# Attention's inverse row sums reach their rows through a small table in device memory

## The chip, the cores and the metric

The kernel runs on one core of one Trainium2 chip. The metric is the time of one execution on the device in microseconds (us), the median of the runs made. An engine here is one of TensorE (PE, whose weight loads are listed apart as PEld), VectorE (DVE), ScalarE (ACT), GpSimd (POOL) and SyncE (SP), which issues nearly all plain DMAs.

## The reference, cut to what matters

A cross attention with eight heads, over channels of 64 rows, and then a mixture of experts. The change is in the attention alone.

```
def _L0_xattn_ref(q, k, v, gamma):          # B, 512, 512 each; q is the normed x, k = v = context
    qh, kh, vh = (a.reshape(B, 8, 64, 512) for a in (q, k, v))
    qk = einsum('bhdq,bhdl->bhql', qh, kh) / sqrt(64)
    sm = softmax(qk, axis=-1)
    ret = einsum('bhql,bhdl->bhdq', sm, vh).reshape(B, 512, 512)
    return gamma * ret
x = x + _L0_xattn_ref(layernorm(x), ctx, ctx, gamma)
x = x + ffn(layernorm(x), ...)              # shared expert, router, top 2 of 8 experts
```

The softmax is computed without its division: each query's exponentials are multiplied with the values, and the result is multiplied by the inverse of that query's sum (and by gamma) afterwards. The queries of a result are its columns, in the free dimension, while the sums come out with the queries on the partitions. So 512 inverse sums for each head have to be turned from columns into rows and repeated over the 64 rows of the head.

## The kernel before, in words

The rows of x (2048) are cut into 16 tiles of 128 rows, two heads each. The first stage handles one tile in one step; the loop is `step(i)`, written once for each engine, with i from -4 to 18, and each engine runs its own list in order, with semaphores between them. Several tiles are in flight in a step: PE computes the scores of tile i and the start of i+1 (`scores`, L1295), transposes the exponentials (`probs_T`, L1315), multiplies them by the values in a high and a low part (`times_v`, L1323), and transposes the normed result of tile i-3 for the router (`rows_T`, L1351, and `logits`, L1357). ACT computes the exponentials (`exps`, L717) and copies the transposed ones out of PSUM (`probs_hi`, L724); DVE takes maxima (L986), the low parts (`probs_lo`, L997) and adds the two halves of a result (`halves`, L1001). POOL splits queries and keys into high and low parts, scales the attention's result (`scaled`, L572) and adds it to x (`residual`, L578). After the 16 tiles come the shared expert (L1428 to 1467) and the 39 slots of the routed experts.

The sums of tile t travel like this. DVE inverts them (`inverse`, L991: `rinv`, 128 partitions with 4 chunks of queries by 2 heads). POOL's `spread(t)` (L566) repeats each of the 8 columns 64 times into `rspr`, 128x512. PE's `inverses(t)` (L1338) transposes it in four pieces of 128x128 into PSUM bank `bT[1]`; in PE's list it stands in step t+1 between the third and the fourth `times_v` of the tile. ACT's `inverses(t)` (L729) copies the bank to `rgam`, with the factor gamma. POOL's `scaled(t)` (L572) waits for it and for DVE's `halves`, and multiplies `att` by `rgam`.

`bT[1]` is shared: `freed(...)` (L1288) makes PE wait for the latest reader of the bank that it will overwrite, and `a_Rg` is ACT's signal after its copy.

SP's list in a step: store the normed rows of tile i-3 (L355), load context i+2 (L347), store the transposed rows i-3 (L359), load x i+4 (L342), store x2 of tile i-1 (L351), and in some steps load weight chunks (L371) or a block of four transposed tiles (`load_block`, L374, 1 MB). In step 16 (i == NT) POOL also makes the high and low parts of weight chunk 1 (`first_weights`, L584), ahead of `scaled(15)`.

Of the kernel before, what the change touches and what calls it, by code (L numbers as in the profile page):

```python
# [5 lines left out]
ALU = mybir.AluOpType  # L6
ACT = mybir.ActivationFunctionType
AX_X = mybir.AxisListType.X
F32 = mybir.dt.float32
# [8 lines left out]
def xattn_moe_kernel(nc, x, ctx_in, gamma, router_w, w_gate, w_up, w_down, sw_gate, sw_up, sw_down, shared_gate_w, out):  # L18
# [49 lines left out]
    xn_d = nc.dram_tensor("x2_normed_rows", (T + P, H), F32, kind="Internal").ap()  # L68
    xT_d = nc.dram_tensor("x2_normed_transposed", (NT, P, H), F32, kind="Internal").ap()
    meta_d = nc.dram_tensor("slot_rows", (SLOTS * P, 2), I32, kind="Internal").ap()  # L70

    ctx = ExitStack()
    with ctx:
        def sem(name):
            return ctx.enter_context(nc.semaphore(name))
# [61 lines left out]
        att = [place(f"att{j}", [P, L]) for j in range(2)]  # L137
        rspr = place("rspr", [P, 2 * QC, DH])
        rgam = place("rgam", [P, L])
# [100 lines left out]

        e_s, d_max, a_exp, d_rinv, g_rspr, e_R, a_Rg = sem("e_s"), sem("d_max"), sem("a_exp"), sem("d_rinv"), sem("g_rspr"), sem("e_R"), sem("a_Rg")

# [53 lines left out]
        def there(t):  # L296

            return not isinstance(t, int) or 0 <= t < NT
# [39 lines left out]
        def _(sp):  # L338
# [14 lines left out]
            def store_normed(t):  # L353
                sp.wait_ge(g_x2n, t + 1)
                sp.dma_start(xn_d[0:T, :].rearrange("(t p) h -> t p h", p=P)[t, :, :], x2n[t % 2][:, :]).then_inc(st_x2n[t % 2], 16)  # L355

            def store_columns(t):
                sp.wait_ge(a_x2T, t + 1)
                sp.dma_start(xT_d[t, :, :], x2T[t % 2][:, :, :].rearrange("p c t -> p (c t)")).then_inc(st_x2T[t % 2], 16)  # L359
# [35 lines left out]
            def step(i):  # L395
                if there(i - 3):
                    store_normed(i - 3)
                if there(i + 2):
                    load_values(i + 2)
                if there(i - 3):  # L400
                    store_columns(i - 3)
                if there(i + 4):
                    load_x(i + 4)
                if i == NT:
                    load_chunk(3)
                if there(i - 1):
                    store_rows(i - 1)
                if i == 2:
                    pads()
                if i == 3:  # L410
                    load_chunk(0)
                if i == 5:
                    load_chunk(1)
                if i == 7:
                    load_block(0, 0)
                if i == 10:
                    load_chunk(2)
                if i == NT - 1:
                    load_block(1, 1)
# [72 lines left out]
        def _(g):  # L492
# [72 lines left out]

            def spread(t):  # L566

                g.wait_ge(d_rinv, t + 1)
                after(g, e_R, t)
                gp.tensor_copy(rspr[:, :, :], rinv[:, :, :].rearrange("p c s -> p (c s)").unsqueeze(2).to_broadcast([P, 2 * QC, DH])).then_inc(g_rspr, 1)  # L570

            def scaled(t):  # L572

                g.wait_ge(d_att, 2 * t + 2)
                g.wait_ge(a_Rg, t + 1)
                gp.tensor_tensor(att[t % 2][:, :], att[t % 2][:, :], rgam[:, :], ALU.mult).then_inc(g_att, 1)
# [23 lines left out]
            def step(i):  # L600
                if there(i + 1):
                    queries(i + 1)
                if there(i + 1) and i + 1 > 0:
                    keys_hi(i + 1)
                    queries_hi(i + 1)
                if there(i - 3):
                    rows_normed(i - 3)
                if i == NT:

                    g.wait_ge(e_s, 8 * NT)  # L610
                    g.wait_ge(e_vt, NT)
                    for n in range(3):
                        first_weights(1, n)
                if there(i + 1) and i + 1 > 0:
                    queries_lo(i + 1)
                    keys_lo(i + 1)
                if 6 <= i < 9:
                    first_weights(0, i - 6)
                if 9 <= i < 9 + TB:
                    first_tokens(i - 9)  # L620
                if there(i - 2):
                    inverse_deviation(1, i - 2)
                if there(i + 2):
                    inverse_deviation(0, i + 2)
                if there(i):
                    spread(i)
                if there(i + 2):
                    shift(0, i + 2)
                if there(i - 1):
                    scaled(i - 1)  # L630
                if there(i - 2):
                    shift(1, i - 2)
                if there(i - 1):
                    residual(i - 1)
# [73 lines left out]
        def _(act):  # L708
# [19 lines left out]

            def inverses(t):  # L729

                act.wait_ge(e_R, t + 1)
                after(act, g_att, t)
                sc.activation(rgam[:, :], bT[1][:, :], ACT.Copy, scale=gam[:, :]).then_inc(a_Rg, 1)

            def low_half(t, s):
# [29 lines left out]
            def step(i):  # L765
# [7 lines left out]
                if there(i - 1):  # L773
                    probs_hi(i - 1, 4)
                    inverses(i - 1)
                    low_half(i - 1, 0)
                    probs_hi(i - 1, 5)
# [178 lines left out]
        def _(dve):  # L956
# [34 lines left out]
            def inverse(t):  # L991

                dve.wait_ge(a_exp, 8 * t + 8)
                after(dve, g_rspr, t)
                ve.reciprocal(rinv[:, :, :], rsum[:, :, :]).then_inc(d_rinv, 1)
# [289 lines left out]
        def _(pe):  # L1285
# [51 lines left out]

            def inverses(t):  # L1338

                pe.wait_ge(g_rspr, t + 1)  # L1340
                for c in range(QC):
                    ins = te.transpose(bT[1][:, c * P:(c + 1) * P], rspr[:, 2 * c:2 * c + 2, :].rearrange("p s d -> p (s d)"), ident[:, :])
                ins.then_inc(e_R, 1)

            def values_T(t, half, par):
# [25 lines left out]
            def step(i, half, par):  # L1371
                if there(i - 1):
                    freed((d_ptl, 8, i - 1, 2), (d_ptl, 8, i - 1, 0), (d_ptl, 8, i - 2, 6), (d_ptl, 8, i - 2, 4))
                    probs_T(i - 1, 1 - par, 4)
                    times_v(i - 1, 1 - par, 2)
                    freed((d_vl, 1, i, 0), (d_ptl, 8, i - 1, 1), (a_x2T, 1, i - 4, 0), (a_Rg, 1, i - 2, 0))
                    inverses(i - 1)
                    times_v(i - 1, 1 - par, 3)
# [7 lines left out]
                if there(i - 3):  # L1386
                    freed((a_Rg, 1, i - 1, 0), (d_vl, 1, i, 0), (d_ptl, 8, i - 1, 1), (a_x2T, 1, i - 4, 0))
                    rows_T(i - 3, 1 - par)
# [14 lines left out]
                if there(i):  # L1403
                    freed((a_x2T, 1, i - 3, 0), (a_Rg, 1, i - 1, 0), (d_vl, 1, i, 0), (d_ptl, 8, i - 1, 1))
                    probs_T(i, par, 1)
# [10 lines left out]
                if there(i + 1):  # L1416
                    freed((d_ptl, 8, i, 1), (a_x2T, 1, i - 3, 0), (a_Rg, 1, i - 1, 0), (d_vl, 1, i, 0))
                    values_T(i + 1, half + par, 1 - par)
# [89 lines left out]
            gate_up(0, 0, 0)  # L1508
            pe.wait_ge(a_Rg, NT)
            rows_T(NT - 2, 0)  # L1510
# [97 lines left out]
```

## Time and profile before

| | before |
|---|---|
| runs | 876.71, 878.79, 879.09 us |
| median | 878.79 us |
| profiled execution, its own time | 879.82 us |
| profiled execution, its span | 878.1 us |
| PE, DVE, ACT, POOL busy in the span | 97%, 65%, 57%, 51% |
| the attention's steady step, from one tile's `inverses` on PE to the next | 13.6 us |

The span reaches from the first to the last instruction of the profiled execution; 1.7 us of that execution's time lie around it. The first stage lasts to about 240 us of the span. The busy time of PE is modelled with the whole duration of each matmul, while matmuls overlap, so the distance from start to start tells more than the busy share.

### The profile page before, as it was taken

The numbers are of one execution on the slowest core, as the hardware profiler recorded it, in microseconds if no ns is written. First come the engines' busy times: TensorE is split into PE (matmuls) and PEld (weight loads), VectorE is DVE, ScalarE is ACT, GpSimd is POOL, SyncE is SP. The second block draws the span as 40 slices with busy tenths as digits, with TensorE's granted clock in tenths as the row PEclk, the third lists the DMA queues.
The fourth block names the chain that finished last, engine by engine and source line by source line (L and its number), as shares of the span: only waits on it lengthen the run. The fifth ranks groups of instructions, "written<-read, shape, count | busy, mean of one in ns | idle before, by whom it ended". The sixth has DMA issues, their size and how long they took to land.

```text
span 878.1 us, 13766 instructions
## 1 busy us (share of the span) xinstructions
PE 849.9 (97%) x4624; PEld 708.6 (81%) x4624; DVE 566.7 (65%) x820; ACT 503.4 (57%) x861; POOL 447.3 (51%) x430
## 2 busy tenths in 40 slices
PE   6999999999999999999999999999999999999993
PEld 3677777777788888888888888888899999999992
DVE  6999999999656414321212121118899999999991
ACT  4899999999653211211111111116788888888881
POOL 5576888875700000144330000003899999999974
PEclk9999999999999999999999999999999999999997
DMA  3124442321453382001320023547744443443442
GB/s 96 61 91 138 133 143 97 132 84 61 156 161 93 85 49 96 1 2 33 112 26 1 0 97 106 191 159 265 216 84 77 85 80 72 81 86 72 76 69 36
DMA packets 63237, 81.24 MB, mean 93 GB/s; under 512 B 15370, under 2 KB 34826, under 8 KB 63187
## 3 DMA queue, kind: packets, MB, share of 16 engines
q1 hardware_dynamic: 53426, 60.14, 22.7%
q0 software_dynamic: 9760, 20.49, 13.1%
q8 instruction: 25, 0.41, 0.2%
q14 instruction: 26, 0.20, 0.1%
HBM read 53.01 MB, written 27.60 MB: 92 GB/s over the span
## 4 chain that ended last, share of the span: by engine, by line
PE 92%; POOL 2%; issue 1%; DMA 1%; DVE 1%; ACT 1%; POOLq 0%; ACTq 0%; DVEq 0%
PE scores L1450 9%; PE scores L1451 9%; PE scores L1452 9%; PE scores L1311 7%; PE bank L1320 6%; PE bank L1464 5%; PE bank L1465 5%; PE bank L1466 5%; PE bank L1334 4%; PE bank L1336 3%; PE bank L1564 3%; PE bank L1565 3%; PE bank L1566 3%; PE bank L1533 3%; PE bank L1535 3%; PE bank L1534 3%
## 5 line engine op out<-in xcount | busy, mean ns | idle before, releaser
L1091 DVE TENSOR_TENSOR sg<-scores,sg 128x512 f32<-128x512 f32 x44 | 30.4, 692 | 201.3 <-PE scores L1452 201.2
L1450 PE MATMUL scores<-x_hl,wsp 128*128 128x512 f32 x352 | 137.2, 390 | 0.0
L1452 PE MATMUL scores<-x_hl,wsp 128*128 128x512 f32 x352 | 137.0, 389 | 0.0
L1451 PE MATMUL scores<-x_hl,wsp 128*128 128x512 f32 x352 | 137.0, 389 | 0.0
L644 POOL DMA_INDIRECT slot_rows<-msrc,posi x32 | 36.1, 1129 | 170.7 <-PE scores L1452 164.3
L659 POOL DMA_INDIRECT xg<-x_normed_rows,meta x39 | 38.5, 988 | 160.0 <-PE scores L1474 141.6
L815 ACT ACTIVATE sg<-scores 128x512 f32<-128x512 f32 x44 | 26.3, 598 | 158.4 <-PE scores L1452 158.4
L822 ACT ACTIVATE hh<-sg 128x512 fp32r<-128x512 f32 x44 | 27.8, 632 | 115.0 <-DVE sg L1091 100.0
L999 DVE TENSOR_TENSOR ptl<-bank,pth 128x512 fp32r<-128x512 f32 x128 | 87.3, 684 | 8.6 <-ACT pth L727 8.1
L721 ACT ACTIVATE pb<-scores,negmax 128x512 f32<-128x512 f32 x128 | 88.1, 694 | 4.6 <-DVE negmax L989 4.6
L727 ACT ACTIVATE pth<-bank 128x512 fp32r<-128x512 f32 x128 | 76.7, 600 | 12.3 <-PE bank L1320 11.1
L685 POOL TENSOR_TENSOR wd<-wex,wd 96x512 fp32r<-96x512 f32 x38 | 79.3, 2087 | 3.2
L1320 PEld LDWEIGHTS bank<-ident,pb 128*128 128x128 f32 x512 | 61.2, 142 | 23.8 <-issue 9.8
L1320 PE MATMUL bank<-ident,pb 128*128 128x128 f32 x512 | 79.7, 280 | 0.2 <-DVE ptl L999 0.2
L989 DVE TENSOR_REDUCE negmax<-scores 128x2 f32<-128x1024 f32 x64 | 77.8, 1215 | 2.9 <-PE scores L1311 2.9
L1452 PEld LDWEIGHTS scores<-x_hl,wsp 128*128 128x128 f32 x352 | 66.1, 188 | 13.8
L1450 PEld LDWEIGHTS scores<-x_hl,wsp 128*128 128x128 f32 x352 | 66.1, 188 | 13.7
L1451 PEld LDWEIGHTS scores<-x_hl,wsp 128*128 128x128 f32 x352 | 66.1, 188 | 13.6
L670 POOL DMA_INDIRECT out<-y,meta x39 | 64.8, 1662 | 16.1 <-DMA out<-y,meta 9.5
L1207 DVE TENSOR_TENSOR wg<-wex,wg 128x1408 fp32r<-128x1408 f32 x39 | 63.5, 1628 | 12.6 <-ACT wg L868 12.5
L1464 PE MATMUL bank<-wsp,hh 128*128 128x512 f32 x176 | 68.8, 391 | 0.8 <-DVE tot_s L1161 0.6
L1466 PE MATMUL bank<-wsp,hl 128*128 128x512 f32 x176 | 68.5, 389 | 0.0
(197 smaller groups left out, 2228.0 us busy)
## 6 DMA issues: line engine op xcount, KB each, us to landing
wex<-in_L_ffn_w_gate SPq DMA_DIRECT2D x8, 704.0 KB, 4.4
wex<-in_L_ffn_w_up SPq DMA_DIRECT2D x8, 704.0 KB, 5.8
xb<-in_x SPq DMA_DIRECT2D x16, 256.0 KB, 2.8
cn<-in_ctx SPq DMA_DIRECT2D x16, 256.0 KB, 2.8
x_rows<-xb SPq DMA_DIRECT2D x16, 256.0 KB, 2.0
x_normed_rows<-x2n SPq DMA_DIRECT2D x16, 256.0 KB, 2.0
x_normed_transposed<-x2T SPq DMA_DIRECT2D x16, 256.0 KB, 2.0
x_hl<-x_normed_transposed SPq DMA_DIRECT2D x4, 1024.0 KB, 5.3
```

Of the source, the lines that this page charges most:

```text
L670: g.indirect_dma_start(out=out, out_offset=bass.IndirectOffsetOnAxis(ap=meta[:, s, 0:1], axis=0), in_=y3[s % 2][:, :], in_offset=None, com ...
L685: gp.tensor_tensor(w[0:IR, 1, c], wex[0:IR, e, 2 * W3 + (IC - 1) * H:EW], w[0:IR, 0, c].bitcast(F32), ALU.subtract).then_inc(g_wd, 1)
L721: sc.activation(pb[t % 2][s][:, c, :], bSS[c % 2][:, s, :], ACT.Exp, bias=negmax[:, c, s:s + 1], scale=1.0, accum_out=rsum[:, c, s:s + 1]) ...
L727: sc.activation(pth[n % 4][:, :], bT[P_BANK[n]][:, :], ACT.Copy).then_inc(a_pth, 1)
L989: ve.tensor_reduce(negmax[:, c, :], bSS[c % 2][:, :, :], AX_X, ALU.max, negate=True).then_inc(d_max, 1)
L999: ve.tensor_tensor(ptl[n % 4][:, :], bT[P_BANK[n]][:, :], pth[n % 4][:, :].bitcast(F32), ALU.subtract).then_inc(d_ptl, 1)
L1320: ins = te.transpose(bT[P_BANK[n]][:, q * P:(q + 1) * P], pb[par][s][:, q, c * P:(c + 1) * P], ident[:, :])
L1450: te.matmul(bk[:, :], hi, xhi, start=(h == 0), stop=False)
L1451: te.matmul(bk[:, :], hi, xlo, start=False, stop=False)
L1452: ins = te.matmul(bk[:, :], lo, xhi, start=False, stop=(h == HC - 1))
L1464: te.matmul(bY[tt][:, :], th, hi, start=(c == 0), stop=False)
L1466: ins = te.matmul(bY[tt][:, :], tl, hi, start=False, stop=(c == SC - 1))
```

## The change

POOL's `spread` becomes `inverses(t)`: one instruction that multiplies the 128x8 inverse sums by gamma into `rgs`. SP stores `rgs` into a table in device memory, `inverse_sums`, with two DMAs for a tile (one for each head, 128 partitions by 4 words, each word going to another place 512 bytes on), and later reads a head's 512 words back as one row, repeated over 64 partitions of `rgam`, with two more DMAs. PE's four transposes, ACT's copy and the waits on `a_Rg` go. The table has two halves, for even and odd tiles.

```diff
+    inv_d = nc.dram_tensor("inverse_sums", (2, 2, L), F32, kind="Internal").ap()
...
-        rspr = place("rspr", [P, 2 * QC, DH])
+        rgs = place("rgs", [P, QC, 2])
...
+            def store_inverses(t):
+
+                sp.wait_ge(g_rgs, t + 1)
+                after(sp, g_att, t - 1)
+                for s in range(2):
+                    sp.dma_start(inv_d[t % 2, s, :].rearrange("(c p) -> p c", p=P), rgs[:, :, s], allow_slow_non_contiguous=True).then_inc(st_inv, 16)
+
+            def load_inverses(t):
+                sp.wait_ge(st_inv, 32 * (t + 1))
+                after(sp, g_att, t)
+                for s in range(2):
+                    sp.dma_start(rgam[DH * s:DH * (s + 1), :], inv_d[t % 2, s, :].partition_broadcast(DH)).then_inc(ld_inv, 16)
...
                 if there(i + 2):
                     load_values(i + 2)
+                if there(i - 1):
+                    load_inverses(i - 1)
                 if there(i - 3):
                     store_columns(i - 3)
                 if there(i + 4):
                     load_x(i + 4)
+                if there(i):
+                    store_inverses(i)
...
-            def spread(t):
+            def inverses(t):
 
                 g.wait_ge(d_rinv, t + 1)
-                after(g, e_R, t)
-                gp.tensor_copy(rspr[:, :, :], rinv[:, :, :].rearrange("p c s -> p (c s)").unsqueeze(2).to_broadcast([P, 2 * QC, DH])).then_inc(g_rspr, 1)
+                after(g, st_inv, 32 * t)
+                if t == 0:
+                    g.wait_ge(ld_small, 48)
+                gp.tensor_scalar(rgs[:, :, :], rinv[:, :, :], gam[:, :], None, ALU.mult).then_inc(g_rgs, 1)
...
                 g.wait_ge(d_att, 2 * t + 2)
-                g.wait_ge(a_Rg, t + 1)
+                g.wait_ge(ld_inv, 32 * (t + 1))
                 gp.tensor_tensor(att[t % 2][:, :], att[t % 2][:, :], rgam[:, :], ALU.mult).then_inc(g_att, 1)
...
-                sc.activation(rgam[:, :], bT[1][:, :], ACT.Copy, scale=gam[:, :]).then_inc(a_Rg, 1)
...
-                    ins = te.transpose(bT[1][:, c * P:(c + 1) * P], rspr[:, 2 * c:2 * c + 2, :].rearrange("p s d -> p (s d)"), ident[:, :])
...
-                    freed((d_vl, 1, i, 0), (d_ptl, 8, i - 1, 1), (a_x2T, 1, i - 4, 0), (a_Rg, 1, i - 2, 0))
-                    inverses(i - 1)
                     times_v(i - 1, 1 - par, 3)
...
-            pe.wait_ge(a_Rg, NT)
```

PE's list before, in a step of the first stage (L1320 is `probs_T`, L1334 and L1336 the two matmuls of one `times_v`, L1342 `inverses`, L1311 `scores`):

```order
L1334 MATMUL bank<-pth_97,vs_90 128x512 [waits a_pth]
L1336 MATMUL bank<-ptl_101,vs_90 128x512 [waits d_ptl]
L1342 MATMUL bank<-ident,rspr 128x128 [waits g_rspr,d_vl]
L1342 MATMUL bank<-ident,rspr 128x128 x3
L1334 MATMUL bank<-pth_98,vs_90 128x512 [waits a_pth]
L1336 MATMUL bank<-ptl_102,vs_90 128x512 [waits d_ptl]
L1320 MATMUL bank<-ident,pb_94 128x128 [waits d_ptl]
```

The same place in the changed kernel (L1334 is now `probs_T`, L1348 and L1350 `times_v`):

```order
L1348 MATMUL bank<-pth_97,vs_90 128x512 [waits a_pth]
L1350 MATMUL bank<-ptl_101,vs_90 128x512 [waits d_ptl]
L1348 MATMUL bank<-pth_98,vs_90 128x512 [waits a_pth]
L1350 MATMUL bank<-ptl_102,vs_90 128x512 [waits d_ptl]
L1334 MATMUL bank<-ident,pb_94 128x128 [waits d_ptl]
```

The four transposes and their wait are gone, and two `times_v` follow each other. Nothing else moves on PE.

SP's list before, at the end of the first stage (from `store_rows(14)` in step 15 on):

```order
L351 DMA x_rows<-xb_87 128x512 [waits g_x2]
L378 DMA x_hl<-x_normed_transposed 128x4x512 [waits st_x2T1,st_x2T0]
L355 DMA x_normed_rows<-x2n_109 128x512 [waits g_x2n]
L359 DMA x_normed_transposed<-x2T_111 128x512 [waits a_x2T]
L371 DMA stg_126<-in_L_ffn_sw_gate 128x4x128 [waits g_wl]
```

The same stretch in the changed kernel, from the two stores of tile 15 on:

```order
L364 DMA inverse_sums<-rgs 128x4x1 [waits g_att,g_rgs]
L364 DMA inverse_sums<-rgs 128x4x1
L353 DMA x_rows<-xb_87 128x512 [waits g_x2]
L393 DMA x_hl<-x_normed_transposed 128x4x512 [waits st_x2T1,st_x2T0]
L357 DMA x_normed_rows<-x2n_109 128x512 [waits g_x2n]
L370 DMA rgam<-inverse_sums 64x512 [waits g_att,st_inv]
L370 DMA rgam<-inverse_sums 64x512
L374 DMA x_normed_transposed<-x2T_111 128x512 [waits a_x2T]
```

The table's loads stand behind the 1 MB load of `x_hl` and the store of the normed rows. In the other steps they stand behind the load of the context, and the stores of the next tile a step's half later, behind the load of x.

## Rows read from the trace of the kernel before

**Rows 1.** The page: span, busy times, and PE's granted clock in 40 slices.
```profile
span 878.1 us, 13766 instructions
...
PE 849.9 (97%) x4624; PEld 708.6 (81%) x4624; DVE 566.7 (65%) x820; ACT 503.4 (57%) x861; POOL 447.3 (51%) x430
...
PEclk9999999999999999999999999999999999999997
```
**Rows 2.** Busy times by stretch (us): PE, PEld, DVE, ACT, POOL, PEclk, DMA share, GB/s.
```profile
120.00:140.00 20.00, 20.00 (x137) 15.00 (x135) 19.27 (x33) 18.34 (x43) 17.72 (x22) 1.00 0.46 157
```
**Rows 3.** The chain that ended last, 120 to 123 us: start, us, what.
```profile
120.90 0.23 PE bank L1336
121.14 0.44 PE bank L1342 x4
121.57 0.23 PE bank L1334
121.81 0.24 PE bank L1336
122.04 0.44 PE bank L1320 x4
```
**Rows 4.** PE's timeline where two `times_v` follow each other: start, us, what.
```profile
225.65 0.39 PE L1336 MATMUL bank<-ptl,vs 128*128 128x512 f32 x1
225.88 0.39 PE L1334 MATMUL bank<-pth,vs 128*128 128x512 f32 x1
226.11 0.40 PE L1336 MATMUL bank<-ptl,vs 128*128 128x512 f32 x1
```
**Rows 5.** All transposes of L1342: duration ns min/median/max, first and last start.
```profile
L1342 PE MATMUL bank<-ident,rspr x64: 271/272/273, 26.2 to 227.7; 128*128 128x128 f32 x64
```
**Rows 6.** The chain where it leaves PE, at the stage's end.
```profile
224.31 0.71 DVE att L1006
225.09 1.30 POOL att L576
```
**Rows 7.** ACT's and DVE's timeline in a steady step, with their idle time before.
```profile
121.61 0.69 ACT L733 ACTIVATE rgam<-bank,gam 128x512 f32<-128x512 f32 x1 [0.31 <-PE bank L1342]
122.32 0.60 ACT L740 ACTIVATE lob<-bank 64x512 f32<-64x512 f32 x1
...
122.95 0.68 DVE L1006 TENSOR_TENSOR att<-bank,lob 64x512 f32<-64x512 f32 x1 [0.17 <-ACT lob L740]
...
128.43 0.69 DVE L999 TENSOR_TENSOR ptl<-bank,pth 128x512 fp32r<-128x512 f32 x1 [0.35 <-ACT pth L727]
```
**Rows 8.** POOL's timeline in the same step, and the scores that wait for its keys.
```profile
122.92 1.28 POOL L557 TENSOR_TENSOR kl<-cn,kh 128x512 fp32r<-128x512 f32 x1
...
125.70 0.50 PE L1311 MATMUL scores<-kh,qh 64*128 64x512 f32 x2
...
128.15 0.61 POOL L570 COPY rspr<-rinv 128x512 f32<-128x512 f32 x1 [0.21 <-DVE rinv L995]
...
128.75 0.26 POOL L528 TENSOR_SCALAR nmr<-aggr,rstd 128x1 f32<-128x1 f32 x1
...
129.94 1.28 POOL L576 TENSOR_TENSOR att<-att,rgam 128x512 f32<-128x512 f32 x1 [0.93 <-DVE att L1006]
```
**Rows 9.** DMA issues of the page: KB each, median us from issue to landing.
```profile
cn<-in_ctx SPq DMA_DIRECT2D x16, 256.0 KB, 2.8
...
x_normed_rows<-x2n SPq DMA_DIRECT2D x16, 256.0 KB, 2.0
...
x_hl<-x_normed_transposed SPq DMA_DIRECT2D x4, 1024.0 KB, 5.3
...
slot_rows<-meta SPq DMA_DIRECT2D x1, 39.0 KB, 17.5
```
**Rows 10.** SP's issues, steady (135.83) and at the stage's end.
```profile
135.83 0.35 SPq L347 DMA_DIRECT2D cn<-in_ctx  x1
...
228.32 1.03 SPq L378 DMA_DIRECT2D x_hl<-x_normed_transposed  x1
229.39 0.51 SPq L355 DMA_DIRECT2D x_normed_rows<-x2n  x1
```
**Rows 11.** Landing of the store issued at 229.39: min/median/max.
```profile
DMA to landing us min/median/max: 5.7/5.7/5.7
```
**Rows 12.** The chain at the stage's end, from POOL back to PE.
```profile
234.91 1.26 POOL att L576
...
239.17 0.77 POOL x2n L564
240.08 0.63 PE bank L1354 x4
```

More of the change, by code:

```diff
@@ L239, in xattn_moe_kernel @@
         e_vt, a_vh, d_vl = sem("e_vt"), sem("a_vh"), sem("d_vl")
-        e_s, d_max, a_exp, d_rinv, g_rspr, e_R, a_Rg = sem("e_s"), sem("d_max"), sem("a_exp"), sem("d_rinv"), sem("g_rspr"), sem("e_R"), sem("a_Rg")
+        e_s, d_max, a_exp, d_rinv, g_rgs = sem("e_s"), sem("d_max"), sem("a_exp"), sem("d_rinv"), sem("g_rgs")
+        st_inv, ld_inv = sem("st_inv"), sem("ld_inv")
         e_t, a_pth, d_ptl, e_pv = sem("e_t"), sem("a_pth"), sem("d_ptl"), sem("e_pv")
@@ L625, in step @@
                 if there(i):
-                    spread(i)
+                    inverses(i)
                 if there(i + 2):
@@ L727, in probs_hi @@
                 sc.activation(pth[n % 4][:, :], bT[P_BANK[n]][:, :], ACT.Copy).then_inc(a_pth, 1)
-            def inverses(t):
-                act.wait_ge(e_R, t + 1)
-                after(act, g_att, t)
-                sc.activation(rgam[:, :], bT[1][:, :], ACT.Copy, scale=gam[:, :]).then_inc(a_Rg, 1)
             def low_half(t, s):
@@ L993, in inverse @@
                 dve.wait_ge(a_exp, 8 * t + 8)
-                after(dve, g_rspr, t)
+                after(dve, g_rgs, t)
                 ve.reciprocal(rinv[:, :, :], rsum[:, :, :]).then_inc(d_rinv, 1)
@@ L1336, in times_v @@
                 te.matmul(bO[:, :], v, ptl[n % 4][:, :], start=False, stop=(c == LC - 1)).then_inc(e_pv, 1)
-            def inverses(t):
-                pe.wait_ge(g_rspr, t + 1)
-                for c in range(QC):
-                    ins = te.transpose(bT[1][:, c * P:(c + 1) * P], rspr[:, 2 * c:2 * c + 2, :].rearrange("p s d -> p (s d)"), ident[:, :])
-                ins.then_inc(e_R, 1)
             def values_T(t, half, par):
@@ L1375, in step @@
                     times_v(i - 1, 1 - par, 2)
-                    freed((d_vl, 1, i, 0), (d_ptl, 8, i - 1, 1), (a_x2T, 1, i - 4, 0), (a_Rg, 1, i - 2, 0))
-                    inverses(i - 1)
                     times_v(i - 1, 1 - par, 3)
@@ L1386, in step @@
                 if there(i - 3):
-                    freed((a_Rg, 1, i - 1, 0), (d_vl, 1, i, 0), (d_ptl, 8, i - 1, 1), (a_x2T, 1, i - 4, 0))
+                    freed((d_vl, 1, i, 0), (d_ptl, 8, i - 1, 1), (a_x2T, 1, i - 4, 0))
                     rows_T(i - 3, 1 - par)
@@ L1403, in step @@
                 if there(i):
-                    freed((a_x2T, 1, i - 3, 0), (a_Rg, 1, i - 1, 0), (d_vl, 1, i, 0), (d_ptl, 8, i - 1, 1))
+                    freed((a_x2T, 1, i - 3, 0), (d_vl, 1, i, 0), (d_ptl, 8, i - 1, 1))
                     probs_T(i, par, 1)
@@ L1416, in step @@
                 if there(i + 1):
-                    freed((d_ptl, 8, i, 1), (a_x2T, 1, i - 3, 0), (a_Rg, 1, i - 1, 0), (d_vl, 1, i, 0))
+                    freed((d_ptl, 8, i, 1), (a_x2T, 1, i - 3, 0), (d_vl, 1, i, 0))
                     values_T(i + 1, half + par, 1 - par)
```

## The prediction

> **What bounds the kernel now.** I read the page first. PE is busy for 97% of the span and its clock is granted in full but for the last slice [rows 1], so the change can only pay through PE's own list, or cost by making PE wait. The view by stretches says the same of the stage that is changed: in 20 us of the first stage PE is busy for 20.00, DVE for 19.27, ACT for 18.34 and POOL for 17.72, at clock 1.00 [rows 2]. The reader should see two things there: PE is full, and DVE is nearly full behind it. Third, the chain that ended last: in steady steps it stays on PE from matmul to matmul, the four transposes of L1342 among them, with 0.44 us [rows 3]. It stays there until DVE's `halves` at 224.31, which hands it to POOL [rows 6], and comes back to PE with `rows_T` at 240.08 [rows 12]. From there on PE works through both expert stages, in which the change touches nothing.
>
> **What is removed from PE.** The transposes are 64 matmuls of 0.272 us [rows 5], 17.4 us of busy time, but matmuls overlap. What counts is how much later the next one starts. With the transposes, the chain gets from the start of the L1336 before them (120.90) to that of the L1334 behind them (121.57) in 0.67 us, of which L1336 has 0.23 and the four transposes 0.44 [rows 3]. Where two `times_v` follow each other without transposes, their starts are 0.23 apart, and 0.23 again [rows 4]. So taking the four out gives 0.44 per tile, and nothing is left in their place.
>
> The Trainium skill (TensorE: Matmul & The Clock Gate, Part 4: PE-mode transpose) gives about 275 ns for a 128x128 transpose in one kernel's context. The trace agrees with that as a duration (0.272), but by it as a price the 60 transposes on the path would give an estimated 16.5 us; the chain prices them at 0.11 each.
>
> The transposes of tiles 0 to 14 are on the path. Those of tile 15 start after 224.31, where the chain has left PE, and give nothing. Gain: 15 x 0.44 = **6.6 us**.
>
> **Can the others follow?** The steady step is 13.6 us and would become 13.2. ACT loses its copy of 0.69 and the idle 0.31 before it [rows 7], 1.0 us in all against 0.44: it follows with ease. DVE loses nothing. In one step it waits twice, 0.17 before `halves` and 0.35 before the first `probs_lo` [rows 7], 0.52 in all, so it can follow 0.44 and has 0.08 left, if both gaps can close. The first one waits for ACT's `lob`, which stood right behind the removed copy (its end is at 122.30, `lob` starts at 122.32), so it closes. The second waits for ACT behind PE's own transposes of the exponentials, which come 0.44 earlier. I therefore take the full 0.44; the bound below is a step that shortens by the 0.17 alone, 15 x 0.17 = 2.6 us.
>
> **POOL.** 0.61 for the spread becomes a small tensor_scalar over 8 words a partition; the nearest rows are 0.26 (one word) and 0.61 (512 words) [rows 8]. Either way it costs nothing: POOL waits 0.93 us for DVE two instructions later [rows 8]. If that cover went, POOL would still be no later than before.
>
> **The DMAs, steady steps.** A tile issues four: two stores of 512 words and two loads of 128 KB. On SP an issue takes 0.35 [rows 10], 1.4 us of a 13.6 us step, between waits for other engines: hidden. The trace has one DMA in which each descriptor moves a few bytes: `slot_rows<-meta`, 39 KB in pieces of 8 bytes, 4992 of them, 17.5 us to landing; a store of 256 KB in long rows lands after 2.0 [rows 9]. So a piece costs (17.5 - 2.0) / 4992, and 1024 words give 2.0 + 3.2 = 5.2 us. The bounds for the pair are 2.0 and 17.5.
>
> How much time is there? The stores can be issued when the inverse sums are scaled, about 128.45 (128.15 plus 0.3). `load_inverses` stands in SP's next step behind the context's load at 135.83 [rows 10]: 7.4 us for 5.2, so SP hardly waits. The table is wanted by `scaled` one step after 129.94, at 143.56 [rows 8]; a load issued at 136.2 and landing like the context's in 2.8 [rows 9] is there at 139. Queued behind SP's new waits are the store of the transposed rows, the next x (four steps ahead) and the x2 store, none of which is wanted before the next step. Cost: 0, and 4.5 us remain as cover.
>
> **The DMAs, at the stage's end.** Here they are not covered. In step 16 the loads stand behind the 1 MB of `x_hl`, issued at 228.32, and the store at 229.39 [rows 10], and that store took 5.7 us instead of 2.0: it landed at 235.1 [rows 11, 9]. The two table loads come behind it. `scaled(15)` starts at 234.91 with POOL busy up to there, and through `residual` and x2n it releases PE's `rows_T` at 240.08 [rows 12]: what it is late there, PE is late. The extra 256 KB at the rate between the 2.8 us of 256 KB and the 5.3 us of 1 MB [rows 9] are 0.85 us, so landing is at about 236.0 and the cost is **1.1 us**. Bounds: 0, if the loads pass the store, and 235.1 + 2.8 - 234.9 = 3.0. I take 1.1, as the row of the delayed store is the nearest.
>
> **Sum.** Against the profiled execution: 879.8 - 6.6 + 1.1 = 874.3 us. That execution is 1.0 us above the median of the runs shown, 878.79; on the median's scale the forecast is **873.3 us**, 0.63% less. A measurement of this kernel tells about 0.3% from no change, which is 2.6 us: 876.2 to 881.4 counts as the same.
>
> **The rivals.**
>
> *DVE takes PE's place (0.20).* For: DVE is busy 19.27 of 20 us [rows 2], and only 0.08 us a step would remain. If the 0.35 gap doesn't close, for it is latency through ACT, the step shortens by 0.17: 878.8 - 2.6 + 1.1 = 877.3, within 0.3%. If neither closes, 879.9. Against: both gaps end at instructions that come earlier with the change.
>
> *The table comes late in every step (0.12, slower).* The place is `scaled`. The mechanism is the price of single words. From 128.45 to 143.56 there are 15.1 us, of which the load needs 2.8, and POOL may be about 1.5 later before PE feels it: its keys end at 124.2 and the scores that need them start at 125.70 [rows 8]. It decides when the stores take over 13.8 us. If each took the 17.5 us of the only row with scattered pieces, the table would be 5.2 us late and PE 3.7, x 15 tiles = 56 us: 878.8 + 56 = 935 us. Against it: that row moves five times as many pieces. The Trainium skill (DMA: Bandwidth & Descriptors, Rules for kernel authors) has a non-contiguous last dimension lowered to one descriptor per element, and calls a plain DMA with a rearranged pattern 19 times slower than a hardware transpose. The 17.5 us row agrees with the first in kind; an estimate by the second, 19 x 2.0 = 38 us a store, would put this rival far above 935. No row here shows such a factor for 512 words.
>
> *Every transpose held PE for its whole duration (0.02).* Then 60 x 0.272 = 16.3 us go: 878.8 - 16.3 + 1.1 = 863.6. The spacing of 0.44 for four speaks flatly against it [rows 3]. It is how the skill's page, named above, would be read.
>
> The forecast keeps 0.66. That the change would not do what it says can be left out: PE's list shows the transposes gone.
>
> **How the numbers follow.** Faster by over 0.3%: 0.66 + 0.02 = 0.68. Within 0.3%: 0.20. Slower: 0.12. The range must leave out no more than 2 in 10: it leaves out the late table (0.12) and the 863.6 (0.02), and a little at each end. Its low end is the full gain without the cost at the stage's end, 878.8 - 6.6 = 872.2, less the 1.2 us by which such medians scatter: 871.0. Its high end takes in the case of DVE with as little scatter: 878.0.
>
> **What would show it.** Right: the distance between one tile's `scores` and the next falls from 13.6 to 13.2 us; the chain stays on PE; DVE's idle time in a step falls to about 0.1; the stores' landing is near 5 us; `scaled(15)` waits for a DMA by about 1 us. Wrong: a step of 13.4 or more with DVE or ACT as the releaser of PE; `scaled` waiting for `rgam`'s DMA in the steady steps; store landings over 12 us; or SP late with the context, so that keys wait.

## The result, and the profile after

The changed kernel takes **894.29 us** (median of 4 runs, 893.46 to 898.59) against 877.89 us for the kernel before beside it: a ratio of **1.0197** [1.0177, 1.0217], 16.4 us slower. The forecast was 5.5 us faster, so its sign is wrong. 894.29 lies outside the range and between "same" and the 935 us of the rival in which the table comes late.

The page of the changed kernel (its profiled execution took 894.19 us). The rows on span, busy times and clock answer to [rows 1]; the others are the busy tenths of PE and of the DMA engines, the packets, the chain by engine, and the DMA issues with their median landing:

```profile
span 892.4 us, 13684 instructions
...
PE 846.9 (95%) x4560; PEld 702.9 (79%) x4560; DVE 565.8 (63%) x820; ACT 492.9 (55%) x845; POOL 438.2 (49%) x430
...
PE   6998998999979999999999999999999999999993
...
PEclk9999999999989999999999999999999999999997
DMA  3466666664663293000211012556944344344442
...
DMA packets 82691, 85.49 MB, mean 96 GB/s; under 512 B 32777, under 2 KB 52233, under 8 KB 82642
...
PE 76%; DMA 9%; POOL 6%; issue 3%; DVE 3%; ACT 1%; SPq 1%; POOLq 0%; another core or an unknown queue 0%; DVEq 0%; ACTq 0%
...
cn<-in_ctx SPq DMA_DIRECT2D x16, 256.0 KB, 5.7
rgam<-inverse_sums SPq DMA_DIRECT2D x32, 128.0 KB, 3.3
x_rows<-xb SPq DMA_DIRECT2D x16, 256.0 KB, 6.3
x_normed_rows<-x2n SPq DMA_DIRECT2D x16, 256.0 KB, 5.6
```

Read it in this order. PE's 64 transposes are gone (4624 - 4560), yet PE now idles in the first stage: its row of tenths shows 8s and a 7 where every slice was 9. The chain that ended last, 92% PE before, holds 9% DMA and 6% POOL. And look at transfers that the change did not touch: the context's load takes 5.7 us instead of 2.8, the two row stores 6.3 and 5.6 instead of 2.0 ([rows 9], and for `x_rows` the line below from the page before). Same bytes, two to three times as long.

```profile
x_rows<-xb SPq DMA_DIRECT2D x16, 256.0 KB, 2.0
```

The same stretch as [rows 2], and the one after it (us; PE, PEld, DVE, ACT, POOL busy, clock, DMA share, GB/s):

```profile
120.00:140.00 20.00, 20.00 (x135) 14.82 (x135) 19.35 (x31) 18.21 (x45) 14.15 (x19) 1.00 0.71 132
140.00:160.00 20.00, 17.61 (x116) 12.52 (x112) 16.89 (x29) 14.41 (x35) 18.29 (x23) 1.00 0.64 107
```

DMA engines are busy for 0.71 of the time instead of 0.46, and move fewer bytes (132 GB/s against 157). PE is whole in the first stretch and loses 2.4 us in the second: the loss comes in every second tile or so.

The chain of waits where that loss arises (start, us, what), which stayed on PE there before [rows 3]:

```profile
119.82 10.10 DMA inverse_sums<-rgs
129.92 0.02 issue
129.94 0.45 SPq L370
130.39 0.05 issue
130.44 6.66 DMA rgam<-inverse_sums
...
137.23 1.29 POOL att L597
```

The same on POOL's and PE's timelines (L591 is the small scaling, L597 `scaled`, L1361 `rows_T`):

```profile
132.16 0.31 POOL L591 TENSOR_SCALAR rgs<-rinv,gam 128x8 f32<-128x8 f32 x1 [0.24 <-DVE rinv L1009]
...
137.23 1.29 POOL L597 TENSOR_TENSOR att<-att,rgam 128x512 f32<-128x512 f32 x1 [4.52 <-DMA rgam<-inverse_sums]
```
```profile
142.76 0.63 PE L1361 MATMUL bank<-ident,x2n 128*128 128x128 f32 x4 [1.80 <-POOL x2n L583]
...
145.35 0.51 PE L1325 MATMUL scores<-kh,qh 64*128 64x512 f32 x2 [0.59 <-POOL kl L576]
```

The two word stores of one tile land 10.1 us after issue (9.7 to 12.2 us at the four places where the chain passes through them), the load of the table behind them needs 6.7 more, and POOL sits idle 4.52 us for it. Behind `scaled` on POOL stand the residual, the normed rows and the keys of the next tile, so PE waits 1.80 us for x2n and 0.59 us for keys. Over the stage, the list of waits:

```profile
POOL att L597 <- DMA rgam<-inverse_sums: 26.6, 8, 5.7
...
PE bank L1361 <- POOL x2n L583: 9.8, 5, 5.0
```
```profile
SPq L370 <- DMA inverse_sums<-rgs: 40.5, 13, 6.5
```

In 8 of the 16 tiles `scaled` waits for the table, in the other 8 for DVE as before: a late tile shifts everything behind it, and that gives the next table time.

The stage's end, in the chain (to be laid beside [rows 12]):

```profile
233.59 9.74 DMA inverse_sums<-rgs
243.35 0.45 SPq L370
243.85 6.10 DMA rgam<-inverse_sums
249.99 0.09 issue
250.09 1.26 POOL att L597
...
253.61 1.11 PE bank L1361 x4
254.73 0.43 PE scores L1455
```

`scaled(15)` starts at 250.09, where it started at 234.91: 15.2 us later, and the span is 14.3 us longer. So the whole loss is in the first stage. Tile 15 waits for its table longer than any other tile:

```profile
250.09 1.26 POOL L597 TENSOR_TENSOR att<-att,rgam 128x512 f32<-128x512 f32 x1 [5.74 <-DMA rgam<-inverse_sums]
```

A last piece of the loss is the clock: PE waited 4.99 us before 253.61 and was busy for 2.63 of the 6 us from 246 to 252, and its granted clock over 252 to 258 was 0.50 (the 1.2 GHz level). Of its next nine matmuls in the chain eight take 0.43 instead of 0.23 and the ninth 0.33, together 1.7 us more.

### The profile page after: what moved, and what is told of

Its sections match the earlier page's. It is cut to its first block, busy times and chain, and to the rows that moved or that the text cites. A ratio compares the mean times of both kernels' runs of the same rounds, so it can differ in the third digit from the quotient of the medians.

```text
span 892.4 us, 13684 instructions
## 1 busy us (share of the span) xinstructions
PE 846.9 (95%) x4560; PEld 702.9 (79%) x4560; DVE 565.8 (63%) x820; ACT 492.9 (55%) x845; POOL 438.2 (49%) x430
## 2 busy tenths in 40 slices
DMA packets 82691, 85.49 MB, mean 96 GB/s; under 512 B 32777, under 2 KB 52233, under 8 KB 82642
## 4 chain that ended last, share of the span: by engine, by line
PE 76%; DMA 9%; POOL 6%; issue 3%; DVE 3%; ACT 1%; SPq 1%; POOLq 0%; another core or an unknown queue 0%; DVEq 0%; ACTq 0%
PE scores L1455 9%; PE scores L1456 9%; PE scores L1457 9%; DMA inverse_sums<-rgs 5%; PE bank L1469 4%; PE bank L1471 4%; PE bank L1470 4%; DMA rgam<-inverse_sums 4%; PE scores L1325 3%; PE bank L1334 3%; PE bank L1569 3%; PE bank L1568 3%; PE bank L1570 3%; PE bank L1537 3%; PE bank L1538 3%
## 5 line engine op out<-in xcount | busy, mean ns | idle before, releaser
L665 POOL DMA_INDIRECT slot_rows<-msrc,posi x32 | 34.0, 1064 | 174.9 <-PE scores L1457 168.5
L1334 PE MATMUL bank<-ident,pb 128*128 128x128 f32 x512 | 80.1, 280 | 3.7 <-ACT pb L742 3.2
L1334 PEld LDWEIGHTS bank<-ident,pb 128*128 128x128 f32 x512 | 60.9, 142 | 28.4 <-issue 9.9
L1221 DVE TENSOR_TENSOR wg<-wex,wg 128x1408 fp32r<-128x1408 f32 x39 | 63.4, 1626 | 12.2 <-ACT wg L882 12.1
```

The source lines that it names most:

```text
L1334: ins = te.transpose(bT[P_BANK[n]][:, q * P:(q + 1) * P], pb[par][s][:, q, c * P:(c + 1) * P], ident[:, :])
```

## What the word stores did to the DMA engines

One pair of stores by itself, issued at 206.44. The first two rows are the DMA engines' busy tenths and GB/s of the changed kernel from 203 to 217.2 us in 40 slices of 0.355 us, the third the packets in it; then SP's issues in the same place:

```profile
DMA  9987145799715260000000039906000040101000
GB/s 254 352 219 196 46 173 173 202 231 364 271 58 11 2 5 0 0 0 0 0 0 0 0 121 387 127 12 23 6 6 0 0 23 17 12 12 17 0 0 0
DMA packets 1722, 1.18 MB, mean 83 GB/s; under 512 B 1152, under 2 KB 1152, under 8 KB 1721
```
```profile
206.44 0.93 SPq L364 DMA_DIRECT2D inverse_sums<-rgs  x2
210.56 0.33 SPq L353 DMA_DIRECT2D x_rows<-xb  x1
213.19 0.33 SPq L357 DMA_DIRECT2D x_normed_rows<-x2n  x1
217.29 1.09 SPq L370 DMA_DIRECT2D rgam<-inverse_sums  x2
```

The words' packets are recorded up to about 208.3 (slices at 58, 11, 2, 5 GB/s). Then the records are empty for 3 us, though SP's wait for the stores, which ends only with the issue at 217.29, says they aren't done. `x_rows`, issued at 210.56, moves most of its data from 211.2 to 212.2; `x_normed_rows`, issued at 213.19, moves nothing in this stretch. A 256 KB store has 144 packets (128 rows and 16 small ones), so the two can be told apart. The first line is for 211 to 217 us, the second for 217.2 to 218.4:

```profile
DMA packets 145, 0.27 MB, mean 45 GB/s; under 512 B 16, under 2 KB 16, under 8 KB 144
```
```profile
DMA packets 144, 0.26 MB, mean 219 GB/s; under 512 B 16, under 2 KB 16, under 8 KB 144
```

The first is `x_rows`, spread out to nearly 217; the second is the whole of `x_normed_rows`, which starts only when the words are done, 4 us after its issue. So the words' own packets are recorded quickly and *completed* slowly, the transfer behind them is picked up and then drags, and the one behind that is not begun: the pair of word stores takes nearly 11 us here, and what is issued behind it pays.

The Trainium skill (DMA: Bandwidth & Descriptors, Queues, rings and completion order) says that a DMA's semaphore increment is written only after every earlier write of the same DMA engine has landed. This trace agrees with it for `x_rows`: most of its data moves within 2 us of issue, while its median landing went from 2.0 to 6.3 us. It doesn't account for `x_normed_rows`, whose data itself is late. No run separates that rule from other ways in which words could hold a transfer up.

## The experiments

Three theories stood after the first look. **Chain:** store and load in sequence take longer than the time to `scaled`, and the wait for one's own words is the loss. **Contention:** the words delay all other transfers, and it matters little who waits for the words. **Something else:** the load of the table, or DVE as the new bound. Where nothing else is said, the ratio is to the kernel before on the same chip, whose median was 878.3 to 878.5 us.

| kernel | median us | ratio [interval] |
|---|---|---|
| changed kernel | 894.29 | 1.0197 [1.0177, 1.0217] |
| a_once | 870.77 | 0.9914 [0.9899, 0.9929] |
| b_loads | 872.50 | 0.9937 [0.9922, 0.9952] |
| c_unread | 894.46 | 1.0184 [1.0156, 1.0211] |
| d_onehead | 883.45 | 1.0079 [1.0050, 1.0108] |
| e_spread | 871.96 | 0.9933 [0.9914, 0.9952] |
| f_dense | 872.74 | 0.9935 [0.9919, 0.9951] |
| g_sbuf | 872.19 | 0.9933 [0.9917, 0.9949] |
| h_mini | 872.70 | 0.9930 [0.9916, 0.9944] |
| l_perm | 888.65 | 1.0120 [1.0092, 1.0148] |
| m_spread16 | 871.49 | 0.9919 [0.9902, 0.9936] |
| o_spread8 | 872.28 | 0.9931 [0.9905, 0.9956] |
| n_perm | 870.36 | 0.9908 [0.9891, 0.9925] |

### First set: which part of the change costs

**a_once.** The table goes out and comes back for tile 0 alone.

```diff
-                if there(i - 1):
+                if i == 1:
                     load_inverses(i - 1)
...
-                if there(i):
+                if i == 0:
                     store_inverses(i)
```

> The changed kernel with the table stored for tile 0 alone and read back once; every tile is scaled by tile 0's sums, and the other tiles' sums are left out. No DMA of the table is left in the steady steps. All theories that blame the table's DMAs say the removal of the four transposes shows alone: 15 x 0.44 = 6.6 us less than before, about 871 us, with a step of 13.2 us. The rival that VectorE takes TensorE's place says 876 or more and a step of at least 13.45 us.

870.77 us, 7.6 us less than before. In its chain the logits (`L1368`, once a tile) start every 13.17 us, against 13.6:

```profile
109.74 0.79 PE bank L1368 x8
...
122.91 0.79 PE bank L1368 x8
...
136.07 0.79 PE bank L1368 x8
```

This is the change without its DMAs. DVE is busy 19.51 of the 20 us from 120 to 140 and still lets PE be busy for 20.00; from 114 to 128 it waits once, for 0.18 us. So the gain on PE is real, and DVE doesn't take its place.

**b_loads.** All 32 loads stay; words are stored for tiles 0 and 1 only.

```diff
-                if there(i):
+                if i == 0 or i == 1:
                     store_inverses(i)
```

> The changed kernel with the word stores of tiles 0 and 1 alone, but all 32 loads of the table; the sums of the later tiles are left out. If the word stores are the cause (by their late landing or by the engines that they hold), this is as fast as without any table DMA, within 1.5 us of 871. If the loads (32 x 128 KB) are the cause, it stays near 890.

872.50 us, 1.7 us over a_once, though the two intervals touch. At the stage's end `scaled(15)` waits 0.98 us for its table, and itself takes 2.25 us instead of 1.3. The second line is DVE in the same place:

```profile
229.39 2.25 POOL L597 TENSOR_TENSOR att<-att,rgam 128x512 f32<-128x512 f32 x1 [0.98 <-DMA rgam<-inverse_sums]
```
```profile
228.74 1.76 DVE L1038 TENSOR_TENSOR wsp<-stg,wsp 128x1536 fp32r<-128x1536 f32 x1 [1.07 <-ACT wsp L773]
```

`scaled(15)` ends 1.14 us after that DVE instruction, and 1.15 us after the same one in m_spread16, as if it had stood still until then. In the kernel before and in a_once the small instruction for `nmr` behind `scaled(15)` is the one that is long there, 1.78 us instead of 0.26 (in the kernel before from 236.15, while that DVE instruction runs from 235.71 to 237.79), so the 2.25 us are no cost of the loads. From the start of `scaled(15)` to the end of x2n it is 5.1 us in a_once and 4.5 in b_loads. What is left of the loads' price is the wait.

What is left between b_loads and the changed kernel, 21.8 us, is the word stores. In the profiles of both the first `halves` starts at 27.6 us, and the last one at 242.9 instead of 227.0 us, and from there to `scaled(15)` it is 7.2 us instead of 2.4: some 16 us arise in the steady steps and 5 at the stage's end.

**c_unread.** All word stores stay, but from tile 2 on they go to a second table that nothing reads; the loads wait for nothing later than tile 1. Two `rgs` buffers, so that the scaling waits only for the stores of two tiles earlier.

```diff
+inw_d = nc.dram_tensor("unread_sums", (2, 2, L), F32, kind="Internal").ap()
...
-                sp.wait_ge(st_inv, 32 * (t + 1))
+                sp.wait_ge(st_inv, 32 * min(t + 1, 2))
```

> All word stores are issued, but from tile 2 on into a second table that nobody reads, with two buffers of the scaled sums, so that nothing waits for their landing within two steps; the loads read the table of tiles 0 and 1. The later tiles' sums are left out. Theory of the chain (store lands after 10 to 12.6 us, SyncE waits, load, scaling: longer than a step): 871 to 875 us. Theory of contention (the words hold up the other transfers on the same 16 engines, whatever is waited for): 885 or more, with x, context and x2 landings of 5 to 6 us.

894.46 us: all of the loss, with no load waiting for the words. So the chain theory isn't needed for the loss, and contention is enough. That the wait would cost nothing by itself isn't shown: no run has as long a wait without the contention. The chain of c_unread shows how the loss comes about without the wait: the issue of the load itself is stretched, and then it lands after 7.2 us.

```profile
129.17 3.58 SPq L375
132.75 0.05 issue
132.80 7.19 DMA rgam<-inverse_sums
140.04 0.10 issue
140.13 1.30 POOL att L609
```

**d_onehead.** Words of one head only, 512 a tile; both halves of `rgam` are read from them.

```diff
-                for s in range(2):
+                for s in range(1):
                     sp.dma_start(inv_d[t % 2, s, :]...
```

> Only the first head's 512 words are stored per tile, and both loads read them; the second head's sums are left out. Everything waits as in the changed kernel. Theory that each word has its price in the landing: the store lands after about 6 us, half of 10 to 12, which is within a step, so 871 to 876 us. If the landing is a fixed price of a DMA with scattered words, it stays at 10 us or more and the time near 894.

883.45 us, a value between those written down. It is 11.0 us above b_loads, where 1024 words are 21.8 above. But the landing doesn't halve. The chain has the store of 512 words at 8.5 to 10.0 us:

```profile
114.73 8.54 DMA inverse_sums<-rgs
...
155.44 9.95 DMA inverse_sums<-rgs
```

So neither theory of the landing holds: not a price for each word (about 6 us), and not quite a fixed one, for the pair takes 9.7 to 12.2. Nor does half the loss make a rule per word. From the first `halves` to the last it is 205.9 us, 6.5 more than in b_loads (199.4), where the changed kernel has 15.9 more (215.3); but at the stage's end `scaled(15)` still waits 5.0 us, against 5.7.

### Second set: what about the words costs

All but h_mini are c_unread with another destination or shape of the unread stores; only the differing line is shown.

**e_spread.** The same 1024 single words, 64 bytes apart.

```diff
+inw_d = nc.dram_tensor("unread_sums", (2, 2, L, 16), F32, kind="Internal").ap()
...
+sp.dma_start(inw_d[t % 2, s, :, 0].rearrange("(c p) -> p c", p=P), rgs[t % 2][:, :, s], ...)
```

> As c_unread, but each unread word goes to a place of its own 64 bytes from the next, where before 16 neighbouring words, written by several of the DMA engines, shared 64 bytes. If neighbours that share a stretch of memory are why a word takes some 100 ns, the landings get short and the time falls to 871 to 876 us. If each scattered word has its price wherever it goes, it stays at 890 to 898 us.

871.96 us: the loss is gone. Packets are as many as in c_unread (82691 in both). So neither the count of pieces nor their 4 bytes by themselves cost 22 us; where they land does.

**f_dense.** The same 4 KB in 128 rows of 32 bytes.

```diff
+sp.dma_start(inw_d[t % 2, 64 * s:64 * (s + 1), :], rgs[t % 2][64 * s:64 * (s + 1), :, :].rearrange("p c s -> p (c s)"))
```

> As c_unread, but the unread store moves the same 4 KB in 128 rows of 32 bytes, 64 rows to a DMA, so 8 pieces per DMA engine and tile in place of 64. If the number of pieces sets the price, it falls to 871 to 876 us with landings near 2.5 us. If any narrow write to device memory stalls the engines for a fixed time, it stays above 885.

872.74 us. 128 adjacent pieces of 32 bytes are harmless; they are also fewer than the words.

**g_sbuf.** The same words into one SBUF row, adjacent, in 8 DMAs of 128 words a tile. SP also waits here for the words of the tile before.

```diff
+for c in range(QC):
+    sp.dma_start(rrow[0:1, s, c, :], rgs[t % 2][:, c, s:s + 1], ...)
```

> As c_unread, but the unread words go to one row in SBUF, in eight DMAs of 128 words per tile, so with four times as many issues on SyncE. If the completion of word writes to device memory is what holds the engines, the transfers behind them run as fast as without words: 871 to 880 us, the context landing after about 3 us. If it is the handling of single words as such, or their issue, it stays at 890 or more.

872.19 us. Adjacent words are harmless in SBUF, in DMAs of 128: it takes device memory as well.

The landings of the unread stores (KB each, median us), in e_spread and in g_sbuf; for stores of adjacent words in device memory the profile gives none, and SP's wait for them in the changed kernel stands for it:

```profile
unread_sums<-rgs SPq DMA_DIRECT2D x28, 2.0 KB, 2.2
```
```profile
rrow<-rgs SPq DMA_DIRECT2D x112, 0.5 KB, 2.0
```

**h_mini.** A full computation: one PE transpose of the 128x8 scaled sums, a copy of 8 rows by ACT, and a store of 8 rows of 512 bytes; the loads stand right behind the row store of the same step.

```diff
+te.transpose(bT[2][0:2 * QC, P:2 * P], rgs[:, :, :].rearrange("p s c -> p (s c)"), ident[:, :])
...
+sc.activation(rT[t % 2][0:2 * QC, :], bT[2][0:2 * QC, P:2 * P], ACT.Copy)
...
+sp.dma_start(inv_d[t % 2, :, :].rearrange("s (c p) -> (s c) p", p=P), rT[t % 2][0:2 * QC, :])
```

> A version meant to beat both: the sums are turned by a single transpose of 128x8 on TensorE (in the bank of the router's logits), copied by ScalarE as 8 rows, stored as 8 rows of 512 bytes, and read back by the same two broadcast loads, issued before the 1 MB load at the stage's end. The whole computation is kept. If only the words are at fault: 0.11 us of TensorE per tile in place of 0.44 and the loads' share as in b_loads, so 873 to 875 us, under the kernel before. If narrow stores or the round trip through memory are at fault as such: 880 or more.

872.70 us, 0.7% under the kernel before: the table in memory works when it isn't written word by word.

### Third set: which neighbours, and how far

**l_perm.** c_unread with adjacent words, but the four words of one partition next to each other (in c_unread neighbours in memory come from neighbouring partitions).

```diff
-inw_d[t % 2, s, :].rearrange("(c p) -> p c", p=P)
+inw_d[t % 2, s, :].rearrange("(p c) -> p c", p=P)
```

> As c_unread, with the same 1024 single words per tile into the same dense 2 KB per head, but a partition's four words stand next to each other, so the 16 words of 64 bytes come from 4 neighbouring partitions instead of 16. If what costs is that words in the same 64 bytes are in flight from several DMA engines at once, and an engine takes whole groups of neighbouring partitions, this falls to about 872 us with landings near 2.2. If it is enough that many words go to the same 64 bytes, whoever sends them, it stays at 885 to 895.

888.65 us. Some 5.8 us less than c_unread, but 16 above b_loads: most of the price doesn't hang on which partition sends the neighbour.

**m_spread16** and **o_spread8.** e_spread with words 16 and 8 bytes apart.

```diff
+inw_d = nc.dram_tensor("unread_sums", (2, 2, L, 4), F32, kind="Internal").ap()
```
```diff
+inw_d = nc.dram_tensor("unread_sums", (2, 2, L, 2), F32, kind="Internal").ap()
```

> As c_unread, with the unread words 16 bytes apart: 4 words in 64 bytes instead of 16 (c_unread) or 1 (e_spread). If the price grows with the number of words in the same 64 bytes: a landing of some 4 to 5 us and a time between 873 and 880. If it depends on several engines in the same 64 bytes: as e_spread, 872 us and about 2.2 us.

> As c_unread, with the unread words 8 bytes apart: 8 words in 64 bytes, between 16 (c_unread, 894 us) and 4 (m_spread16, 871 us). If the price of a word grows with its neighbours in the same 64 bytes, this lies between: 873 to 888 us, with transfers behind the words landing later than in m_spread16. If one more gap is enough to free them, 871 to 872 us.

871.49 and 872.28 us: both free. A store lands after 3.6 us at 16 bytes and 4.3 at 8, against 2.2 at 64, so closeness does cost the store something, but far less than adjacency, and the row stores are back (in o_spread8 `x_rows` lands after 2.2, in c_unread after 5.5). The context's load is not quite: 4.0 us in both, 3.3 in b_loads. One unused word between two words is enough. My theory of how many words share a block of 64 bytes would have left a part of the loss at 16 bytes, and more at 8; it falls.

**n_perm.** A full computation without any PE work: the four words of a partition and head are stored as one piece of 16 bytes, pieces adjacent, in partition order, and `scaled` reads the row in permuted order. The loads stand behind the row store, as in h_mini.

```diff
-rgs = place("rgs", [P, QC, 2])
+rgs = place("rgs", [P, 2, QC])
...
+sp.dma_start(inv_d[t % 2, :, :].rearrange("s (p c) -> p s c", c=QC), rgs[:, :, :]).then_inc(st_inv, 16)
...
+a3 = att[t % 2][:, :].rearrange("a (c p) -> a c p", p=P)
+gp.tensor_tensor(a3, a3, rgam[:, :].rearrange("a (p c) -> a c p", c=QC), ALU.mult).then_inc(g_att, 1)
```

> The whole computation, without any transpose on TensorE: the table is stored in the order in which the partitions hold it (a partition's four sums of a head next to each other, 16 bytes a piece, 256 pieces in one DMA), read back as rows, and GpSimd reads rgam in the permuted order when it scales. Loads issued before the 1 MB load. If only the crowded single words were at fault, this keeps the removal's gain less the price of the loads: 871 to 873 us, the fastest complete version. If GpSimd's strided read costs more than its 0.9 us of waiting per step, or narrow neighbours still stall the engines, 876 or more.

870.36 us, ratio 0.9908 [0.9891, 0.9925], the fastest kernel of the study; its interval overlaps h_mini's. From POOL's timeline, and the store's median landing:

```profile
125.14 1.56 POOL L597 TENSOR_TENSOR att<-att,rgam 128x512 f32<-128x512 f32 x1 [1.02 <-DVE att L1020]
```
```profile
inverse_sums<-rgs SPq DMA_DIRECT2D x16, 4.0 KB, 2.2
```

The permuted read makes `scaled` 1.56 us instead of 1.28, and the wait for DVE before it covers that. The same 4 KB land after 2.2 us where words took 10. These are 256 pieces, a quarter of the words; even 512 words a tile cost 11.0 us in d_onehead, so the fewer pieces hardly explain it, though no run has 1024 touching pieces of 16 bytes. At the stage's end `scaled(15)` follows POOL's own work at 227.3 and waits for no DMA, where b_loads waits 0.98 us: the loads' new place, ahead of the 1 MB load, takes back the cost that the forecast saw there.

## Why the prediction was wrong

- **What is removed from PE, 15 x 0.44 = 6.6 us: right.** a_once gains 7.6 us with an interval of 6.2 to 8.9 (0.9929 and 0.9899 of 878.38), and the step is 13.17. The spacing of starts was the price, not the 0.272 us of a transpose.
- **The others follow: right.** DVE closed its gaps; the rival in which it takes PE's place (0.20) falls by a_once, where PE is busy for 20.00 of 20 us.
- **POOL: right.** The small tensor_scalar takes 0.31 us, between the bounds of 0.26 and 0.61, and is hidden.
- **The stage's end, 1.1 us: right without the words.** With steady steps undisturbed (b_loads) `scaled(15)` waits 0.98 us for the table; b_loads minus a_once is 1.7, not clear of noise. In the changed kernel this term is swamped by the words of tile 15 (9.74 + 6.10 us in the chain, a wait of 5.74).
- **So the sum was right but for the words:** b_loads, which has every other term, takes 872.50 us against the 873.3 forecast.
- **"The DMAs, steady steps. Cost: 0": this step failed**, and twice. First, the landing of the stores came from `slot_rows<-meta` as a price of 3.1 ns for each piece, (17.5 - 2.0) / 4992, giving 5.2 us for the pair; it was 9.7 to 12.2 us in the chain. The bounds of 2.0 and 17.5 hold it, but a price for each piece is not how the words behave: 512 of them took 8.5 to 10.0 us (d_onehead). And the price came from a single row, whose DMA lands after 11.9 to 18.0 us over the kernels here. Second, and worse, the step took the stores' time as a private matter of the table: if the load was in time, nothing was lost. The sum had no term for what the words do to the transfers behind them. By b_loads the word stores cost 21.8 us in place of 0, and c_unread shows that their traffic alone is enough for all of it.
- **The rival of the late table (0.12): right in place and sign, wrong in its point of decision and its price.** It wanted stores over 13.8 us. They took 10.1 at 120 us, but the load behind them took 6.7 instead of 2.8, together 16.8 against the 15.1 that it allowed. By its own sum PE would then lose 1.7 - 1.5 = 0.2 us a step, 3 us in all. The trace has more: POOL was ready 13.3 us after the sums (119.38 to 132.71) and waited 4.52, and eight tiles waited 3.3 us on average. The change came to 16.4 us, neither 3 nor 56. That c_unread loses as much without waiting for its words shows that the rival's mechanism, the wait for one's own stores, isn't needed.
- **The rule of the Trainium skill** against this change (DMA: Bandwidth & Descriptors, Rules for kernel authors: a non-contiguous last dim becomes one descriptor per element, and a rearranged plain DMA is 19 times slower than a hardware transpose) was set aside because no row of before bore it out. The packets agree with its first half: 82691 after, 63237 before. For the second half no hardware transpose was run. The estimate of 38 us took the factor over a row store of 2.0; the words took five to six times that. That a rearranged store can be slow fits the changed kernel, and e_spread doesn't fit it: as many one-word pieces, landing after 2.2 us, and no loss.

What would have made the forecast right is a question and not a number: not only when the stores land, but what is queued behind them on the same queue in that time. Here it was the load of x, the context, both row stores and the table's own load.

**Still open.** Why words that touch in device memory are slow and words with a gap of 4 bytes are not: no run looks inside the memory. `slot_rows<-meta` moves touching pieces of 8 bytes and takes 17.5 us [rows 9]; nothing was tried that splits that DMA's time, so whether 8-byte pieces that touch pay as well isn't known. All transfers that were seen to suffer stood behind the words on SP's queue; no run issues the words from another engine, so whether they hold that queue, the DMA engines or the memory isn't shown. How much of the loss is the stretched issue on SP and how much the late landing isn't separated either. That `scaled(15)` or `nmr` stands still for DVE's instruction is read from the times in the traces; no run moves that instruction.

## What to carry to other kernels

A DMA that writes single words next to one another into device memory is not priced by its bytes or by its own landing. Lay it out in larger pieces and let the reader undo the permutation: with pieces of 16 bytes the same table was free here (n_perm, 870.36 us, against 870.77 for a_once, which has nearly none of the table's DMAs). When a change adds a DMA of an untested shape, list every transfer that is issued in the microseconds after it and ask what each may lose; the sign of that in a profile is that the landings of untouched transfers grow while GB/s falls and the DMA share rises. To find out whether a transfer hurts by its waiters or by its traffic, keep the traffic and take away the reader.

## What the runs showed of the hardware that was not expected

- 1024 adjacent 4-byte stores into device memory land after 9.7 to 12.2 us, 512 of them after 8.5 to 10.0, while their packet records end after some 2 (206.44 to 208.3). The records are then empty for 3 us. So the busy share shows nothing of the gap, though over 20 us it is higher than before (0.71 against 0.46).
- A store behind the words moved most of its data at once and landed late; the next one moved none until the words were done (issued at 213.19, its 144 packets after 217.2).
- The same words land after 2.2, 3.6 and 4.3 us (512 a DMA) at a pitch of 64, 16 and 8 bytes, with the row stores back at 2.0 to 2.2 and the context's load at 3.9 to 4.0 instead of 3.3, and the kernel at 871.5 to 872.3 us; at a pitch of 4 bytes they cost it 22 us.
- Adjacent words into SBUF (872.19 us), and pieces of 32 bytes (872.74) or 16 bytes (870.36) into device memory, cost the kernel nothing that can be told from noise.
- Issuing a DMA can itself stall: in c_unread the pair of loads that stood behind the words took 4.22 us to issue, 1.09 us where nothing was in the way.
